# Mamba block with adaptive norms: layer norms on ScalarE, two additions on GpSimd, two PSUM banks in the last feed-forward, state sum two units behind the scans

## The chip, the cores and the metric

The kernel runs on one core of a Trainium2 chip. The metric is the device time of one launch in microseconds (us). The engines are TensorE (PE; its weight loads are listed as PEld), VectorE (DVE), ScalarE (ACT), GpSimd (POOL) and SyncE (SP), which issues the DMA transfers. Each runs its own instruction stream in order and waits for others by semaphores.

## The reference, cut to what matters

16 samples of 512 positions by 256 features go through a bidirectional Mamba block (512 channels, 64 states each) and a feed-forward, each with a scaled and shifted norm in front and a gate behind.

```python
h = layernorm(x) * (1 + ca) + sa
xn = layernorm(h, ln1)                          # the kernel's x_norm, then h_norm
x1 = mamba(xn, m1); x2 = flip(mamba(flip(xn), m2))
x = x + ga * (layernorm(x1 + x2, ln2) + xn)     # o_norm, then mix
n = layernorm(x) * (1 + cb) + sb                # n_norm
h = silu(n @ w1) * (n @ w2); h = gelu(h @ h1); h = gelu(h @ h2)
x = x + gb * (h @ w3)                           # W0, W1

# inside mamba, over t, for each of 512 channels and 64 states n:
h[t] = exp(dt[t] * A) * h[t-1] + dt[t] * x[t] * B[t]
y[t] = sum_n h[t] * C[t]
y = (y + xc * D) * silu(z)
```

## The kernel before, in words

The recurrence over time is one DVE instruction per 128 x 1024 values (`tensor_tensor_scan`). The work of a sample is cut into 128 **units**: two directions, four chunks of 128 channels, 16 groups of four states. A unit has two halves of 1024 values in a row. The samples follow each other as **bodies** of one program: `pre` (only the projections of sample 0), `first`, fourteen `mid` bodies (a loop), `last`, and `tail` (what is left of sample 15: output projection, norms, the whole feed-forward, no scans).

In each unit:

- ACT computes the decays `exp(dt * A)` of unit + 2 into one of four `state` slots (`decays`, L1034), and in two portions the products `v` for a later odd unit (`make_v`, L1047). POOL computes the last quarter of `v` (L1320).
- The driving term `driven` (a PSUM ring of two halves) comes from DVE for even units (`drive`, L1216) and from PE for odd units, by transposes of `v` (`drive`, L857). PE's transposes of a half wait for the scan of the same half of the unit before.
- DVE scans both halves in place (`scan`, L1227).
- POOL multiplies the scanned state by C (`read`, L1257).
- PE sums over n into `y_ps` (`accumulate`, L871). That frees the `state` slot: `decays` of unit + 2 wait for `summed` of unit - 2 (`slot_free`). At PE's unit u the code calls `accumulate(u - 1)` between the transposes of the two halves.
- SP loads the C rows, `ud` rows and weights.

After 16 units, DVE adds `xc * D` to `y_ps` (step `Y`, L1145), and the first `accumulate` of the next 16 waits for it.

All else (projections of the other direction and of the next sample, and norms and feed-forward of the previous sample) is laid out as **side steps** by a table: `side_steps` gives each step a unit, and each engine's `side` issues a step at the end of that unit. The step lists are per engine, so a step of engine A that needs one of engine B waits for B's count. A norm is four steps (`norm_steps`): `stats` (DVE, unit s), `aggr` (DVE, s + 1), `rstd` (POOL, s + 2, seven small instructions, L1274 to L1280), `norm` (DVE, s + 3, four `tensor_scalar` of 128 x 256, L1168). The four norms start at o: 8, n: 18, x: 64, h: 71. `x_scale` (L1172) and `x_shift` (L1174) follow at 68 and 69. `mix0` (L1177) and `mix1` (L1180) are DVE steps at 15 and 16. `W0` and `W1` (L1185 and L1188) are two DVE instructions each, at 76 and 127. The gates (POOL, L1288) are at 1 and 65.

The feed-forward works on 256 positions at a time with one PSUM bank, `q_ps`: PE fills it (L799 for F, L812 for H and G, L822 for W), ACT reads it (L1002, L1012), and `bank_free` holds PE's next step until ACT has read.

## Time and profile before

| what | value |
|---|---|
| median of 3 runs | 13444.66 us (13441.17 to 13444.91) |
| the profiled execution | 13442.57 us, of which the span is 13440.8 us |
| DVE busy | 12440.7 us (93%) |
| POOL busy | 11452.0 us (85%) |
| ACT busy | 10728.5 us (80%) |
| PE busy | 10269.7 us (76%), mean granted clock 0.877 |
| DMA | 1450 MB, about a third of the 16 engines' time |

The page gives busy time by engine; the windows view gives it by stretch; the list of waits says what ended an engine's idle time; the lines view groups instructions by source line; the timeline shows them in order. A timeline row is start, length, engine, line, operation, tiles, shape, count, and in brackets the idle time before it and what ended it.

### The profile page before, as it was taken

The page shows a single profiled execution, that of the slowest core. Times are in us where ns is not written, and L with a number is a line of the kernel's source. Part 1 is how long each engine was busy: PE and PEld are TensorE (multiplying, and loading weights), DVE is VectorE, ACT ScalarE, POOL GpSimd, SP SyncE. Part 2 cuts the span into 40 slices and gives each one's busy share as a digit, 9 for nine tenths or more (in the row PEclk, how much of TensorE's full clock was granted, in tenths as well). Part 3 has the DMA queues.
Part 4 walks back from the last instruction along what each step waited for, and adds up shares of the span by engine and source line. Part 5 has one row for each costly group of instructions (what it writes and reads, how often), then busy time and mean ns, then how long its engine had stood idle before and what let it go on. Part 6 is the DMA issues. An engine that isn't in the chain of part 4 may idle for free.

```text
span 13440.8 us, 178922 instructions
## 1 busy us (share of the span) xinstructions
PE 10269.7 (76%) x51228; PEld 5835.9 (43%) x51228; DVE 12440.7 (93%) x7383; ACT 10728.5 (80%) x23196; POOL 11452.0 (85%) x5812
## 2 busy tenths in 40 slices
PE   5567877778787787877878777787877878778776
PEld 2234444444344444434444444443444444344445
DVE  5999999999999999999999999999999999999991
ACT  5788878888887887878888788888878878788882
POOL 4898888888888888888988888888888888889892
PEclk7778988889898898988989888898988989889898
DMA  2223333333333333333333333333333333333332
GB/s 84 79 88 106 107 106 118 116 102 117 98 121 106 110 118 103 119 103 114 118 106 107 106 118 116 104 118 96 122 106 112 116 102 119 103 114 120 102 108 87
DMA packets 605372, 1450.00 MB, mean 108 GB/s; under 512 B 68400, under 2 KB 109504, under 8 KB 599792
## 3 DMA queue, kind: packets, MB, share of 16 engines
q1 hardware_dynamic: 604272, 1437.26, 32.8%
q8 instruction: 455, 7.45, 0.2%
q14 instruction: 645, 5.28, 0.1%
HBM read 1346.70 MB, written 90.31 MB: 107 GB/s over the span
## 4 chain that ended last, share of the span: by engine, by line
PE 26%; ACT 25%; issue 21%; DVE 17%; POOL 11%; DMA 0%; DVEq 0%; POOLq 0%; ACTq 0%; SPq 0%
DVE state L1227 9%; ACT v_sb L1047 8%; ACT state L1034 8%; PE driven L857 8%; POOL state L1257 8%; PE y_ps L871 5%; PE q_ps L812 5%; DVE driven L1216 3%; PE q_ps L799 2%; PE p_ps L720 2%; PE b_ps L847 1%; ACT L1034 1%; POOL v_sb L1320 1%; PE p_ps L728 1%; ACT hid L1017 1%
## 5 line engine op out<-in xcount | busy, mean ns | idle before, releaser
L1257 POOL TENSOR_TENSOR state<-state,c_rep 128x1024 f32<-128x1024 f32 x4096 | 9661.5, 2382 | 1544.2 <-DVE state L1227 1543.4
L1227 DVE TENSOR_TENSOR_SCAN state<-state,driven 128x1024 f32<-128x1024 f32 x4096 | 9105.9, 2270 | 462.7 <-PE driven L857 245.8
L1047 ACT ACTIVATE v_sb<-u_t,b_t 128x128 f32<-128x128 f32 x12288 | 3978.2, 505 | 1764.3 <-PE driven L857 1759.3
L1034 ACT ACTIVATE state<-ud_rep,cols_sb 128x512 f32<-128x512 f32 x8192 | 5175.6, 709 | 3.0 <-DMA ud_rep<-ud_rows 0.8
L857 PE MATMUL driven<-consts_sb,v_sb 128*128 128x128 f32 x16384 | 2700.5, 319 | 2119.8 <-DVE state L1227 2089.2
L857 PEld LDWEIGHTS driven<-consts_sb,v_sb 128*128 128x128 f32 x16384 | 2184.9, 164 | 3778.6 <-DVE state L1227 2605.4
L871 PE MATMUL y_ps<-state,consts_sb 128*32 128x512 f32 x16384 | 2523.6, 693 | 372.1 <-POOL state L1257 369.4
L1216 DVE TENSOR_TENSOR driven<-ud_rep,b_ps 128x1024 f32<-128x1024 f32 x2048 | 2390.0, 1212 | 17.0 <-DMA ud_rep<-ud_rows 17.0
L812 PE MATMUL q_ps<-hid,wq_sb 128*128 128x256 f32 x8192 | 2132.6, 406 | 241.1 <-ACT hid L1012 152.2
L812 PEld LDWEIGHTS q_ps<-hid,wq_sb 128*128 128x128 f32 x8192 | 1534.3, 197 | 982.8 <-issue 750.2
L1320 POOL TENSOR_TENSOR v_sb<-u_t,b_t 128x512 f32<-128x512 f32 x1024 | 1181.7, 1154 | 11.4 <-ACT u_t L963 11.4
L871 PEld LDWEIGHTS y_ps<-state,consts_sb 128*32 128x32 f32 x16384 | 341.9, 115 | 1178.2 <-issue 602.5
L728 PE MATMUL p_ps<-u_pad,dt_sb 128*128 128x512 f32 x1024 | 541.3, 655 | 40.7 <-ACT u_pad L939 40.2
L799 PE MATMUL q_ps<-xn_q,wq_sb 128*128 128x256 f32 x2048 | 529.5, 403 | 44.9 <-ACT hid L1002 40.5
L720 PE MATMUL p_ps<-x_t,wp_sb 128*128 128x512 f32 x1024 | 500.0, 611 | 24.1 <-ACT sz L983 12.5
L847 PE MATMUL b_ps<-b_parts,onehot 32*128 32x512 f32 x1024 | 517.7, 506 | 0.0
L799 PEld LDWEIGHTS q_ps<-xn_q,wq_sb 128*128 128x128 f32 x2048 | 378.0, 194 | 226.4 <-issue 125.6
L1012 ACT ACTIVATE hid<-q_ps,cols_sb 128x256 f32<-128x256 f32 x512 | 237.2, 463 | 293.8 <-PE q_ps L812 293.8
L822 PE MATMUL q_ps<-wq_sb,hid 128*128 128x256 f32 x1024 | 282.4, 424 | 51.8 <-ACT hid L1017 44.7
L728 PEld LDWEIGHTS p_ps<-u_pad,dt_sb 128*128 128x128 f32 x1024 | 192.1, 201 | 266.6 <-issue 197.5
L720 PEld LDWEIGHTS p_ps<-x_t,wp_sb 128*128 128x128 f32 x1024 | 187.3, 192 | 230.5 <-issue 135.6
L1304 POOL TENSOR_TENSOR hid<-hid 128x1024 f32<-128x1024 f32 x64 | 151.2, 2364 | 158.0 <-ACT hid L1006 158.0
(121 smaller groups left out, 5616.7 us busy)
## 6 DMA issues: line engine op xcount, KB each, us to landing
c_rep<-bc_rows SPq DMA_DIRECT2D x2048, 256.0 KB, 3.0
ud_rep<-ud_rows SPq DMA_DIRECT2D x512, 512.0 KB, 4.1
wq_sb<-in_h SPq DMA_DIRECT2D x512, 512.0 KB, 3.8
wq_sb<-in_f SPq DMA_DIRECT2D x128, 512.0 KB, 4.0
wp_sb<-in_win SPq DMA_DIRECT2D x64, 512.0 KB, 4.8
dt_sb<-conv_taps SPq DMA_DIRECT2D x32, 1024.0 KB, 5.6
ud_rows<-u_pad SPq DMA_DIRECT2D x128, 256.0 KB, 3.5
ud_rows<-dt_sb SPq DMA_DIRECT2D x128, 256.0 KB, 3.4
```

The costliest lines, as they stand in the source:

```text
L720: mm = pe.matmul(p_ps[:], wp_sb[:, m, k, :], x_t[:, k, :], start=(k == 0), stop=(k == DC - 1))
L728: mm = pe.matmul(p_ps[:], conv_w[:, m, k, :], u_pad[:, m, k:k + T], start=(k == 0), stop=(k == TAPS - 1))
L799: mm = pe.matmul(q_ps[:, which * TH:(which + 1) * TH], w[:, m % 2, which, k, :], n_t[:, k, i * TH:(i + 1) * TH], start=(k == 0), stop=(k = ...
L812: mm = pe.matmul(q_ps[:, 0:TH], w[:, k, :], src[:, k, :], start=(k == 0), stop=(k == HC - 1))
L857: mm = pe.transpose(driven[:, q % DRIVE_RING, j % 2, tt * P:(tt + 1) * P], v_sb[:, unit // 2 % V_RING, tt, j].rearrange("p e n -> p (e n)" ...
L871: mm = pe.matmul(y_ps[EG * j:EG * (j + 1), :], over_nn, state[:, k % STATE_RING, j, :], start=(g == 0), stop=(g == NG - 1))
L1034: ins = act.activation(state[:, unit % STATE_RING, j, :], ud_rep[:, nth % 2, j, 1, :], ACT.Exp, scale=a_neg[:, d, c, j, g:g + 1])
L1047: ins = act.activation(v_sb[:, unit // 2 % V_RING, tt, :, :, n].rearrange("p j e -> p (j e)"), u_t[:, nth % 2, tt, :], ACT.Identity, scale ...
L1216: dve.tensor_tensor(driven[:, h], u_rows(unit)[:, 2 * h:2 * h + 2], b_ps[:].unsqueeze(1).to_broadcast([P, 2, T]), ALU.mult).then_inc(dve_d ...
L1227: dve.tensor_tensor_scan(flat, flat, driven[:, q % DRIVE_RING].rearrange("p j t -> p (j t)"), 0.0, ALU.mult, ALU.add).then_inc(scanned, 1)
L1257: pool.tensor_tensor(part, part, c_rep[:, unit % ROW_RING, :].unsqueeze(1).to_broadcast([P, 2, T]), ALU.mult).then_inc(was_read, 1)
L1320: pool.tensor_tensor(v_sb[:, unit // 2 % V_RING, TT - 1].rearrange("p j e n -> p (j e) n"), u_t[:, nth % 2, TT - 1, :].unsqueeze(2).to_bro ...
```

## The change

- **Norms.** The four `norm` steps move from DVE to ACT, at the same units: four `activation(Identity)` per norm with `scale = rstd` and `bias = -mean * rstd`. POOL's `rstd` step has two more small instructions for that bias. `x_scale` and `mix` on DVE now wait for ACT.
- **Additions.** `x_q += o_sb` (was `mix1`, DVE, unit 16) becomes POOL's step `mixed` in unit 16; the second instruction of `W0` and `W1` becomes POOL's `add0` and `add1` in the same units. ACT's first F step waits for the addition, since it overwrites `hid2`; `n_stats` waits for `mixed`.
- **Two banks.** In the tail alone the feed-forward steps alternate between `q_ps` and `p_ps`, and `bank_free` looks two steps back.
- **Sum.** PE's unit u calls `accumulate(u - 2)`, always behind the transposes of the first half; bodies after the first one sum two units of the body before.
- **Y and gates.** `Y` steps and both gates come one unit later.

```diff
-    dve = [(s, part, name + "_stats", TT), (s + 1, part, name + "_aggr", TT), (s + 3, part, name + "_norm", TT)]
+    dve = [(s, part, name + "_stats", TT), (s + 1, part, name + "_aggr", TT)]
...
-    return [(s + 2, part, name + "_rstd", 7)], dve
+    return [(s + 2, part, name + "_rstd", 9)], [(s + 3, part, name + "_norm", TT)], dve
...
-        dve.append((NG * (c + 1), "o0", f"Y0{c}", 1))
-        dve.append((NG * (EC + c + 1), "o0", f"Y1{c}", 1) if c < EC - 1 else (0, "early", f"Y1{c}", 1))
-    pool.append((1, "early", "gate1", 2))
+        dve.append((NG * (c + 1) + 1, "o0", f"Y0{c}", 1))
+        dve.append((NG * (EC + c + 1) + 1, "o0", f"Y1{c}", 1) if c < EC - 1 else (1, "early", f"Y1{c}", 1))
+    pool.append((2, "early", "gate1", 2))
...
-    dve += [(MIX_AT + i, "early", f"mix{i}", 1) for i in range(2)]
+    dve.append((MIX_AT, "early", "mix", 1))
+    pool.append((MIX_AT + 1, "early", "mixed", 1))
...
-        dve.append((w_at + 4, part, f"W{i}", 2))
+        dve.append((w_at + 4, part, f"W{i}", 1))
+        pool.append((w_at + 4, part, f"add{i}", 1))
...
-    pool.append((NG * EC + 1, "o0", "gate0", 2))
+    pool.append((NG * EC + 2, "o0", "gate0", 2))
...
+        def q_bank(at, part, name):
+
+            if at.kind != "tail":
+                return q_ps
+            return (q_ps, p_ps)[[s[1:3] for s in PE_Q if at.has(s[1]) and s[3]].index((part, name)) % 2]
...
-                if j:
-                    p, n = steps[j - 1][1:3]
+                back = 2 if at.kind == "tail" else 1
+                if j >= back:
+                    p, n = steps[j - back][1:3]
...
-                    before_scans = unit == 0 and at.kind in ("mid", "last", "tail")
-                    to_drive, ends_pass = scans and unit + 1 in PE_UNITS, unit % NG == 0
+                    before_scans = unit < 2 and at.kind in ("mid", "last", "tail")
+                    to_drive, ends_pass = scans and unit + 1 in PE_UNITS, False
                     if to_drive and not ends_pass:
                         drive(at, unit + 1, 0)
-                    if before_scans or scans and unit:
-                        accumulate(at, unit - 1)
+                    if before_scans or scans and unit >= 2:
+                        accumulate(at, unit - 2)
...
+                if name.endswith("norm"):
+                    i = 0 if part == "next" else 1
+                    src, dst = {"o": (o_sb, o_sb), "n": (x_q, o_sb), "x": (xa, xa), "h": (xa, xa)}[name[0]]
+                    act.wait_ge(pool_side.sem, pool_side.done(at, part, name[0] + "_rstd"))
+                    for tt in range(TT):
+                        act.activation(dst[:, tt, :], src[:, tt, :], ACT.Identity, scale=rstd[:, i, tt:tt + 1],
+                                       bias=less_mean[:, i, tt:tt + 1]).then_inc(done, 1)
...
-                    elif name[2:] == "norm":
-                        dve.wait_ge(pool_side.sem, pool_side.done(at, part, kind + "_rstd"))
-                        for tt in range(TT):
-                            emit(dve.tensor_scalar(dst[:, tt, :], src[:, tt, :], mv[:, i, tt, 0:1],
-                                                   rstd[:, i, tt:tt + 1], ALU.subtract, ALU.mult), tt == TT - 1)
...
-                elif name == "mix1":
-                    dve.wait_ge(pool_side.sem, pool_side.done(at, "early", "pre2"))
-                    emit(dve.tensor_tensor(x_q[:], x_q[:], o_sb[:], ALU.add), True)
...
-                    dst = x_q[:, 2 * i:2 * i + 2, :]
-                    emit(dve.tensor_tensor(dst, dst, tmp, ALU.add))
...
+                    emit(pool.tensor_tensor(nb, mean, r, ALU.mult))
+                    emit(pool.tensor_tensor(nb, zero.to_broadcast([P, TT]), nb, ALU.subtract))
...
+                if name.startswith("add"):
+                    i = int(name[3])
+                    pool.wait_ge(dve_side.sem, dve_side.done(at, part, f"W{i}"))
+                    dst = x_q[:, 2 * i:2 * i + 2, :]
+                    pool.tensor_tensor(dst, dst, hid2[:, 0:2, :], ALU.add).then_inc(done, 1)
+                if name == "mixed":
+                    pool.wait_ge(done, pool_side.done(at, part, "pre2"))
+                    pool.wait_ge(dve_side.sem, dve_side.done(at, part, "mix"))
+                    pool.tensor_tensor(x_q[:], x_q[:], o_sb[:], ALU.add).then_inc(done, 1)
```

## Rows read from the trace of the kernel before

**Rows 1.** Windows: length, busy (count) of PE, PEld, DVE, ACT, POOL; clock; DMA

```profile
4000.00:8000.00 4000.00, 3108.72 (x15645) 1770.64 (x15647) 3816.74 (x2259) 3280.14 (x7082) 3505.19 (x1780) 0.88 0.34 111
...
5110.95:5117.85 6.90, 0.00 (x0) 0.00 (x0) 5.42 (x4) 4.52 (x8) 5.68 (x8) 0.58 0.04 14
```

**Rows 2.** Waits of DVE, then ACT, 4000 to 8000: total us, times, longest

```profile
DVE state L1227 <- PE driven L857: 68.4, 103, 1.5
DVE state L1227 <- ACT state L1034: 56.3, 45, 2.4
DVE o_sb L1168 <- POOL small L1280: 7.4, 5, 1.5
DVE xa L1168 <- POOL small L1280: 3.4, 5, 0.7
...
DVE state L1227 <- DVE x_q L1180: 1.0, 5, 0.2
...
ACT v_sb L1047 <- PE driven L857: 531.5, 124, 11.0
```

**Rows 3.** Lines of DVE, whole run: busy us, mean ns | idle before

```profile
L1168 DVE TENSOR_SCALAR xa<-xa,small 128x256 f32<-128x256 f32 x128 | 170.1, 1388 | 16.6 <-POOL small L1280 16.6
L1168 DVE TENSOR_SCALAR o_sb<-o_sb,small 128x256 f32<-128x256 f32 x64 | 82.6, 1349 | 24.7 <-POOL small L1280 24.7
L1188 DVE TENSOR_TENSOR x_q<-x_q,hid 128x512 f32<-128x512 f32 x32 | 65.4, 2044 | 1.1
L1168 DVE TENSOR_SCALAR o_sb<-x_q,small 128x256 f32<-128x256 f32 x64 | 59.3, 985 | 2.9 <-POOL small L1280 2.9
```

**Rows 4.** One source line (mix1) without the tail: ns min/median/max, first to last start

```profile
L1180 DVE TENSOR_TENSOR x_q<-x_q,o_sb x15: 2958/2969/2978, 1070.6 to 12489.3; 128x1024 f32<-128x1024 f32 x15
```

**Rows 5.** Timeline of a middle body, o_norm in unit 11

```profile
5112.40 5.42 DVE L1168 TENSOR_SCALAR o_sb<-o_sb,small 128x256 f32<-128x256 f32 x4 [1.45 <-POOL small L1280]
...
5120.19 1.97 PE L857 MATMUL driven<-consts_sb,v_sb 128*128 128x128 f32 x8 [10.37 <-DVE state L1227]
...
5125.92 2.29 DVE L1227 TENSOR_TENSOR_SCAN state<-state,driven 128x1024 f32<-128x1024 f32 x1 [1.43 <-PE driven L857]
```

**Rows 6.** Timeline of a pair of units without DVE side steps (34 and 35)

```profile
5260.39 8.81 DVE L1227 TENSOR_TENSOR_SCAN state<-state,driven 128x1024 f32<-128x1024 f32 x4
...
5263.16 1.04 PE L857 MATMUL driven<-consts_sb,v_sb 128*128 128x128 f32 x8
...
5263.65 2.55 ACT L1034 ACTIVATE state<-ud_rep,cols_sb 128x512 f32<-128x512 f32 x4
5264.14 1.07 PE L871 MATMUL y_ps<-state,consts_sb 128*32 128x512 f32 x8
...
5271.36 4.46 DVE L1227 TENSOR_TENSOR_SCAN state<-state,driven 128x1024 f32<-128x1024 f32 x2
```

**Rows 7.** A line of ACT in the stretch 4000 to 8000 us

```profile
L1012 ACT ACTIVATE hid<-q_ps,cols_sb 128x256 f32<-128x256 f32 x159 | 73.5, 462 | 49.1 <-PE q_ps L812 49.1
```

**Rows 8.** Lines of POOL, whole run

```profile
L1257 POOL TENSOR_TENSOR state<-state,c_rep 128x1024 f32<-128x1024 f32 x4096 | 9661.5, 2382 | 1544.2 <-DVE state L1227 1543.4
L1320 POOL TENSOR_TENSOR v_sb<-u_t,b_t 128x512 f32<-128x512 f32 x1024 | 1181.7, 1154 | 11.4 <-ACT u_t L963 11.4
L1276 POOL TENSOR_TENSOR small<-small 128x4 f32<-128x4 f32 x64 | 13.0, 204 | 5.0
```

**Rows 9.** Timeline of the tail: norm, mix, one F step, one H step, W

```profile
13172.35 1.38 DVE L1168 TENSOR_SCALAR o_sb<-o_sb,small 128x256 f32<-128x256 f32 x4 [2.89 <-POOL small L1280]
...
13175.02 1.23 DVE L1180 TENSOR_TENSOR x_q<-x_q,o_sb 128x1024 f32<-128x1024 f32 x1
...
13195.76 1.99 PE L799 MATMUL q_ps<-xn_q,wq_sb 128*128 128x256 f32 x8 [0.93 <-ACT hid L1002]
...
13236.21 3.72 PE L812 MATMUL q_ps<-hid,wq_sb 128*128 128x256 f32 x16 [0.56 <-ACT hid L1012]
...
13427.36 8.61 PE L822 MATMUL q_ps<-wq_sb,hid 128*128 128x256 f32 x32 [3.52 <-DMA wq_sb<-in_w]
```

More of the change, by code:

```diff
@@ L583, in store_xn @@
             def store_xn(at):
-                wait(dve_side.sem, dve_side.done(at, "next", "h_norm"))
+                wait(act_side.sem, act_side.done(at, "next", "h_norm"))
                 sp.dma_start(rows_of(xn_dram, at.b + 1), xa[:]).then_inc(xn_out.sem, 16)
@@ L599, in store_out @@
             def store_out(at):
-                wait(dve_side.sem, dve_side.done(at, "late", "W1"))
+                wait(pool_side.sem, pool_side.done(at, "late", "add1"))
                 sp.dma_start(rows_of(out, at.b - 1), x_q[:]).then_inc(out_stored.sem, 16)
@@ L705, in project @@
                         if part == "next":
-                            pe.wait_ge(dve_side.sem, dve_side.done(at, "next", "h_norm"))
+                            pe.wait_ge(act_side.sem, act_side.done(at, "next", "h_norm"))
                         else:
-                            pe.wait_ge(dve_side.sem, dve_side.before(at))
+                            pe.wait_ge(act_side.sem, act_side.before(at))
                     for tt in range(TT):
@@ L768, in network @@
             def network(at, part, name, quarter):
-                kind, n = name[0], name[1:]
+                kind, n, bank = name[0], name[1:], q_bank(at, part, name)
                 if quarter == 0:
@@ L784, in network @@
                     if k == 0:
-                        pe.wait_ge(dve_side.sem, dve_side.done(at, part, "n_norm"))
+                        pe.wait_ge(act_side.sem, act_side.done(at, part, "n_norm"))
                     for tt in range(TT):
-                        mm = pe.matmul(q_ps[:, tt * P:(tt + 1) * P], o_sb[:, tt, k * P:(k + 1) * P], ident,
+                        mm = pe.matmul(bank[:, tt * P:(tt + 1) * P], o_sb[:, tt, k * P:(k + 1) * P], ident,
                                        start=True, stop=True)
@@ L798, in network @@
                         for k in range(DC):
-                            mm = pe.matmul(q_ps[:, which * TH:(which + 1) * TH], w[:, m % 2, which, k, :],
+                            mm = pe.matmul(bank[:, which * TH:(which + 1) * TH], w[:, m % 2, which, k, :],
                                            n_t[:, k, i * TH:(i + 1) * TH], start=(k == 0), stop=(k == DC - 1))
@@ L811, in network @@
                     for k in range(4 * quarter, 4 * quarter + 4):
-                        mm = pe.matmul(q_ps[:, 0:TH], w[:, k, :], src[:, k, :], start=(k == 0), stop=(k == HC - 1))
+                        mm = pe.matmul(bank[:, 0:TH], w[:, k, :], src[:, k, :], start=(k == 0), stop=(k == HC - 1))
                 else:
@@ L995, in step @@
                     k = int(name[1])
-                    act.activation(n_t[:, k, :], q_ps[:], ACT.Identity, scale=mod_c[:, DC + k:DC + k + 1],
+                    act.activation(n_t[:, k, :], q_bank(at, part, name)[:], ACT.Identity, scale=mod_c[:, DC + k:DC + k + 1],
                                    bias=mod_c[:, k:k + 1]).then_inc(done, 1)
@@ L1000, in step @@
                     m = int(name[2])
+                    if m == 0 and (name[1] == "1" or at.kind != "first"):
+                        act.wait_ge(pool_side.sem, pool_side.done(at, "early", "add0") if name[1] == "1"
+                                    else pool_side.before(at))
                     for which, hid in enumerate((hid1, hid2)):
-                        act.activation(hid[:, m, :], q_ps[:, which * TH:(which + 1) * TH], ACT.Identity,
+                        act.activation(hid[:, m, :], q_bank(at, part, name)[:, which * TH:(which + 1) * TH], ACT.Identity,
                                        scale=scales[:, which, m:m + 1]).then_inc(done, 1)
@@ L1158, in step @@
                             dve.wait_ge(x_in.sem, x_in.done(at, "next", "x"))
+                        if kind == "n":
+                            dve.wait_ge(pool_side.sem, pool_side.done(at, "early", "mixed"))
                         for tt in range(TT):
```

41 lines of the change are left out of this document (23 added, 18 removed).

## The prediction, made before the result

> **What bounds the kernel now.** I read the windows first. In the stretch from 4000 to 8000 us DVE is busy for 3816.74 of 4000 us, which is 95.4%; POOL has 87.6%, ACT 82.0% and PE 77.7% [rows 1]. So DVE sets the pace there, and the rest of its time can be named: in the list of its waits, 68.4 us end with PE's transposes, 56.3 us with ACT's decays, 10.8 us with POOL's `rstd` [rows 2]. A middle body takes (12489.3 - 1070.6) / 14 = 815.6 us, by the first and the last start of an instruction that occurs once in a body [rows 4]. The stretch is therefore 4.90 bodies. Fourteen such bodies are 11,418 of the 13,441 us. The tail is another matter: there is no scan, and PE and ACT take turns at one bank [rows 9].
>
> An instruction taken from DVE is thus worth its whole duration, as long as the engine that gets it and the waits that it brings stay under DVE's new pace.
>
> **Norms, taken from DVE.** Per body (totals over 16): (170.1 + 82.6 + 59.3) / 16 = 19.5 us [rows 3]. The waits for `rstd` go too: 10.8 / 4.90 = 2.2 us [rows 2]. A norm also stops PE: its transposes wait for a scan, 10.37 us in the place shown, and then take 1.97 us where eight take 1.04 us elsewhere [rows 5, 6]; the granted clock of that pause is 0.58 of 2.4 GHz, nearer the 1.2 GHz level than the upper one [rows 1]. The slow transposes make the scan of unit 13 wait 1.43 us [rows 5]. I count that once per body. A DVE step that waits for its own last write leaves up to 0.2 us before the next scan [rows 2]; seven such waits go with the norms and additions, 0 to 1.4 us, and I take 1.2.
>
> **Additions, taken from DVE.** `mix1` takes 2.97 us [rows 4], and the second halves of `W0`, `W1` 65.4 / 16 = 4.1 us [rows 3]. Together DVE loses 19.5 + 2.2 + 1.4 + 1.2 + 3.0 + 4.1 = **31.4 us per body**.
>
> **What ACT gets.** Four ACTIVATE per norm. One of the same shape takes 462 ns [rows 7], so a norm is at least 1.85 us and four are 7.4 us per body. ACT waits 531.5 / 4.90 = 108 us per body for PE's transposes, in front of `v_sb` [rows 2]. That covers 7.4 us, in the mean. It is not everywhere: where ACT is behind, DVE waits for decays, 56.3 / 4.90 = 11.5 us per body [rows 2]. The norm on ACT also waits for `rstd` in front of the decays of the next unit. By the code those are due two units after they are issued. I cost it at nothing; with that cover gone it is 7.4 us.
>
> The Trainium skill speaks against this move: "ScalarE: Activation LUTs", Rules for kernel authors, gives additions and multiplications to VectorE. In the tail the row agrees, 4 tensor_scalar in 1.38 us against 1.85 us; beside GpSimd's work it does not, since there the same four take 5.42 us [rows 5, 9]. By that rule the norms would be a loss of some 0.5 us each, hidden or not.
>
> **What POOL gets.** One addition of 128 x 1024 and two of 128 x 512: at 2382 ns for 1024 values that is 2.4 + 2.4 us. Two small instructions more per norm at 204 ns plus 5.0 / 64 us between them: 8 x 0.28 = 2.3 us [rows 8]. Sum 7.1 us. POOL's busy time per body is 3505.19 / 4.90 = 715 us; it becomes 722, against a body of some 790 us: 91%. Per pair of units without side work POOL has 4 x 2.38 + 1.15 = 10.7 us (rather less back to back) against DVE's 5271.36 - 5260.39 = 10.97 [rows 6, 8]. So POOL recovers slowly from a burst. The worst one is at unit 66, where the gate (2 x 2.38 us, moved there) now stands in front of `x_rstd`, on POOL's queue: after the scan of unit 66, a last read 2.4, `v` 1.15, the gate 4.8, `rstd` with nine instructions 3.3, then ACT 1.85, 13.5 us in all. DVE reaches `x_scale` in unit 68 after two units, 2 x 4.4 + 2.3 = 11.1 us. That is a **new wait of 2.4 us**, queued behind it on DVE are the scans of unit 69, and for those PE and POOL wait. Other bursts, and DVE's remaining two-input operations beside a busier POOL, I bound by 0 and by 5 us per body (the `x_q` addition takes 1.23 us alone in the tail and 2.97 us in a body [rows 4, 9]; three further such operations could lose 1.7 us each) and take 2.5.
>
> The Trainium skill, "GPSIMD Engine Reference", Engine selection, says that an elementwise operation with two inputs is about twice as slow on GpSimd and belongs on VectorE. The tail agrees (1.23 us on DVE, 2.4 us by POOL's mean), so there the move costs. If it held on the path of the bodies too, the sum would lose the 7.0 us of the additions per body, about 100 us in all.
>
> **The sum two units behind.** Before, PE's `accumulate` stands between the transposes of the two halves and needs POOL's read of the unit before. Now it needs a read that is one unit older, so PE waits less for POOL; no row shows DVE gaining by it, and I take nothing. It has a price: a `state` slot comes free later, and ACT's decays wait for that. In the pair shown the decays start at 5263.65; with the sum of two units earlier in the place of this one, they would start when it ends, 5264.14 + 1.07 = 5265.21, that is 1.56 us later [rows 6]. Where ACT is behind anyway it comes later than that sum and loses nothing. DVE's waits for ACT's decays are 45 in 4.90 bodies, 9 per body, so the cost is between 0 and 9 x 1.56 = 14 us per body. Nearer the low end: ACT waits for PE in only 124 / 4.90 = 25 of a body's 64 pairs [rows 2]; in between it works without a pause, and a late start is then paid once for several waits of DVE, or by ACT's own next pause. I take **2.2 us**, one and a half times 1.56.
>
> **Y and gates later.** `Y` (0.7 us) only moves, and PE's next `accumulate` is later too. `gate1` at unit 2 ends 2.4 + 1.15 + 4.8 = 8.3 us after the scan of unit 2; PE's `O1a` waits for it at unit 3, with the transposes for unit 5 queued behind it. Those are due 4.4 + 2.3 + 4.4 = 11.1 us after that scan; `O1a` and one half take about 2 to 3 us. It just fits; if not, 1 us per body, inside the bound above.
>
> **A body** then saves 31.4 - 2.4 - 2.5 - 2.2 = **24.3 us**: 14 x 24.3 = 340. The first body has only x and h norms (10.6 + 0.7 us, less 2.4 and 1): 8. The last has o, n and the additions (8.9 + 1.5 + 7.0 + 1.4, less 4): 15.
>
> **Tail.** An F step takes 1.99 + 0.93 us, PE and then ACT; an H or G step 3.72 + 0.56 us [rows 9]. With two banks PE goes on. Between steps of one phase there are 7 intervals: F 2 x 7 x 0.93 = 13 (and up to 0.2 more each, as matmuls flow on); H and G 4 x 7 x 0.56 = 16, and up to 0.2 each by the same. Weights could hold this: PE waited 3.52 us for the last chunk [rows 9], and a slot's next chunk may be asked for only when its step is done, one step of 3.5 us ahead. That just covers it. The pair of N steps and the pair of O steps each lose one such gap, some 0.9 us: 2. I take 13 + 16 + 5 + 2 = 36, bounds 15 and 40. Against it: two norms on ACT (0.5 each), `rstd` (0.6 each), `mixed` 2.4 for 1.23, the adds 0.5 each: 4. Net 32, and the projection of sample 0 loses 2.
>
> **Sum.** 340 + 8 + 15 + 32 - 2 = 393. From the profiled 13442.6 us that gives 13,050; the median of the runs is 2 us above it, which is nothing here. **Predicted: 13,050 us.**
>
> **Rivals.**
>
> - *Nothing is lost elsewhere.* 31.4 us per body, 440 + 12 + 19, and 37 of the tail: 12,935. For it: POOL and ACT have room in the mean. Against it: DVE waits for them now. Chance 0.15.
> - *Half is eaten by new waits.* POOL is at 91% and late in bursts, ACT's backlog is paid five times: 12 us per body, 168 + 10 + 20: about 13,245, or 13,160 if the gain is 18 us. Chance 0.20.
> - *The norms only filled holes.* DVE's pauses gave POOL and ACT the time to catch up, and it now waits as long for `read` and decays: no gain in the bodies, 20 us in the tail. Speaks for it: POOL's 10.7 against 10.97 us. Against it: 108 us of ACT's and a tenth of POOL's time are idle. 13,425. Chance 0.04.
> - *Slower: the late sum starves ACT.* Place: `slot_free` in front of the decays. Price 1.56 us for each pair of units in which ACT has no room. It decides from 33 / 1.56 = 21 pairs of the 64 per body on. With 30 pairs: 47 us lost against 31.4, 15.6 us per body, some 218 us less the tail's 32: 13,630 (rounded). Against it: ACT must have been just in time in each of them, and only 9 waits per body show that. Chance 0.08.
>
> The forecast's own case (13,050, from 12,970 to 13,130) has 0.53. The range reaches from 12,925 to 13,260 and takes in the second and third case. A measurement of this kernel tells some 0.2% from no change. Faster by more than that: 0.88; within it 0.04; slower 0.08.
>
> **What would show it right or wrong.** No DVE row for the norms, body period near 791 us, DVE's busy share still about 95%. `x_scale` (DVE) waiting for ACT, some 2.4 us, once per body. DVE's waits for decays 11.5 us per body before: 14 if I am right, over 40 if the last rival is. F steps of the tail every 2 us, H every 3.5 to 3.7. If ACT waits at its decays for PE's `y_ps` in most pairs, but DVE not for ACT, the late sum costs nothing.

## The result, and the profile after

| | before | after |
|---|---|---|
| median (lowest to highest), same chip | 13443.57 us (13441.17 to 13444.91) | 13064.94 us (13057.31 to 13073.71) |
| profiled execution, its span | 13442.57, 13440.8 us | 13063.83, 13062.0 us |
| busy share of PE, DVE, ACT, POOL | 76, 93, 80, 85% | 78, 92, 83, 88% |

The ratio is 0.9719, with a 95% interval from 0.9702 to 0.9736: faster, 15 us from the forecast of 13,050.

Windows of the kernel after, with the columns of [rows 1]:

```profile
4000.00:8000.00 4000.00, 3171.38 (x16098) 1811.82 (x16097) 3769.79 (x2221) 3405.99 (x7382) 3639.71 (x1883) 0.90 0.35 113
...
5610.83:5621.46 10.63, 0.01 (x2) 0.01 (x1) 10.42 (x7) 6.10 (x17) 6.60 (x3) 0.64 0.05 8
```

DVE's share went from 95.4 to 94.2% [rows 1], although it has less to do: it waits more. Single lines of the kernel after, whole run or without the tail (ns min/median/max, first and last start): the step `mix`, which occurs once in a body, and the scan:

```profile
L1197 DVE TENSOR_TENSOR o_sb<-o_sb,mod_q x15: 1225/3030/5386, 1059.6 to 12146.2; 128x1024 f32<-128x1024 f32 x15
```

```profile
L1242 DVE TENSOR_TENSOR_SCAN state<-state,driven x4096: 2258/2262/2290, 171.5 to 12802.2; 128x1024 f32<-128x1024 f32 x196
```

A middle body takes (12146.2 - 1059.6) / 14 = 791.9 us, against 815.6 [rows 4]. The last scan starts at 12802.2, so the tail is 13062.0 - 12802.2 - 2.3 = 257.5 us; before, the last scan started at 13144.7 of 13440.8 and the tail took 293.8. From the starts of every 256th scan the span divides like this (us):

| | start | first body | 14 middle bodies | last body | tail |
|---|---|---|---|---|---|
| before | 167.7 | 791.8 | 14 x 815.66 | 768.2 | 293.8 |
| after | 171.5 | 791.4 | 14 x 791.67 | 758.1 | 257.6 |
| difference | +3.8 | -0.4 | -335.8 | -10.2 | -36.2 |
| foretold | +2 | -8 | -340 | -15 | -32 |

The same instructions of DVE also changed their durations. Three of them, over 128 x 2048 values, belong to the making of dt. First the kernel before, then after; columns as in [rows 3]. `rest` writes `u_pad`, `dt` writes `dt_sb`, `log1p` writes `sz`; the last line is `x_scale`:

```profile
L1197 DVE SCALAR_TENSOR_TENSOR u_pad<-sz,u_pad 128x2048 f32<-128x2048 f32 x32 | 141.7, 4428 | 55.2 <-ACT sz L975 55.2
L1203 DVE TENSOR_TENSOR dt_sb<-dt_sb,sz 128x2048 f32<-128x2048 f32 x32 | 116.9, 3653 | 1.1
L1201 DVE TENSOR_TENSOR sz<-sz,u_pad 128x2048 f32<-128x2048 f32 x32 | 81.2, 2536 | 36.5 <-ACT sz L978 36.5
```

```profile
L1212 DVE SCALAR_TENSOR_TENSOR u_pad<-sz,u_pad 128x2048 f32<-128x2048 f32 x32 | 91.8, 2870 | 52.2 <-ACT sz L992 52.2
L1218 DVE TENSOR_TENSOR dt_sb<-dt_sb,sz 128x2048 f32<-128x2048 f32 x32 | 97.0, 3030 | 1.1
L1216 DVE TENSOR_TENSOR sz<-sz,u_pad 128x2048 f32<-128x2048 f32 x32 | 95.8, 2993 | 55.5 <-ACT sz L995 55.5
L1191 DVE TENSOR_TENSOR xa<-xa,mod_p 128x1024 f32<-128x1024 f32 x16 | 19.9, 1244 | 36.5 <-ACT xa L939 36.5
```

Waits of DVE, of ACT and of PE in the kernel after, 4000 to 8000 us, as in [rows 2]:

```profile
DVE state L1242 <- PE driven L867: 97.4, 116, 2.7
DVE state L1242 <- ACT state L1054: 69.3, 50, 2.8
...
DVE xa L1191 <- ACT xa L939: 10.7, 5, 2.2
```

```profile
ACT state L1054 <- PE y_ps L881: 505.4, 204, 9.7
```

```profile
PE q_ps L790 <- POOL u_pad L1306: 17.5, 5, 3.7
```

The stretch holds 4000 / 791.9 = 5.05 bodies. Per body DVE waits 19.3 us for transposes (14.0 before), 13.7 for decays (11.5 before) and 2.1 for the norm in front of `x_scale`. The waits for `rstd` are gone. ACT's large wait is now at its decays, for PE's sum, and no longer at `v_sb`.

### The profile page after: what moved, and what is told of

Same layout as the page of the kernel before. It is cut to its first block, busy times and chain, and to the rows that moved or that the text cites. A ratio compares the mean times of both kernels' runs of the same rounds, so it can differ in the third digit from the quotient of the medians.

```text
span 13062.0 us, 179154 instructions
## 1 busy us (share of the span) xinstructions
PE 10161.7 (78%) x51228; PEld 5798.5 (44%) x51228; DVE 11974.4 (92%) x7080; ACT 10814.2 (83%) x23452; POOL 11547.6 (88%) x5988
## 4 chain that ended last, share of the span: by engine, by line
PE 28%; ACT 26%; issue 20%; DVE 17%; POOL 7%; DMA 1%; DVEq 0%; SPq 0%; POOLq 0%; ACTq 0%
DVE state L1242 10%; PE driven L867 9%; ACT state L1054 9%; ACT v_sb L1067 9%; PE y_ps L881 6%; POOL state L1272 4%; PE q_ps L822 4%; DVE driven L1231 3%; PE q_ps L809 2%; PE p_ps L730 2%; PE b_ps L857 1%; ACT L1054 1%; PE p_ps L738 1%; POOL u_pad L1306 1%; PE p_ps L754 1%
## 5 line engine op out<-in xcount | busy, mean ns | idle before, releaser
L1242 DVE TENSOR_TENSOR_SCAN state<-state,driven 128x1024 f32<-128x1024 f32 x4096 | 9103.8, 2270 | 561.9 <-PE driven L867 325.0
L822 PE MATMUL q_ps<-hid,wq_sb 128*128 128x256 f32 x7936 | 2031.1, 400 | 188.3 <-ACT hid L1032 109.0
L822 PEld LDWEIGHTS q_ps<-hid,wq_sb 128*128 128x128 f32 x7936 | 1463.3, 194 | 892.3 <-issue 699.3
L738 PE MATMUL p_ps<-u_pad,dt_sb 128*128 128x512 f32 x1024 | 511.6, 623 | 44.6 <-ACT u_pad L956 44.3
L775 PE MATMUL p_ps<-sz 16*128 16x512 f32 x256 | 181.8, 796 | 149.2 <-ACT u_pad L986 148.7
```

The source lines that it names most:

```text
L738: mm = pe.matmul(p_ps[:], conv_w[:, m, k, :], u_pad[:, m, k:k + T], start=(k == 0), stop=(k == TAPS - 1))
L822: mm = pe.matmul(bank[:, 0:TH], w[:, k, :], src[:, k, :], start=(k == 0), stop=(k == HC - 1))
L1242: dve.tensor_tensor_scan(flat, flat, driven[:, q % DRIVE_RING].rearrange("p j t -> p (j t)"), 0.0, ALU.mult, ALU.add).then_inc(scanned, 1)
```

## The experiments

Each was timed beside the kernel before, on the same chip as it. "The kernel after" as a base has 13,065 us. Body lengths are first and last start of `mix`, divided by 14, as above; per-unit figures are means over twelve middle bodies, from the starts and ends of the scans. A unit is counted from the start of its first scan to that of the next unit. An interval belongs to a ratio to the kernel before; two runs whose intervals overlap are not told apart by their times alone.

### The parts one by one

**Norms alone.** The kernel before, with the four `norm` steps on ACT and the two further small instructions on POOL.

```diff
-    return [(s + 2, part, name + "_rstd", 7)], dve
+    return [(s + 2, part, name + "_rstd", 9)], [(s + 3, part, name + "_norm", TT)], dve
```

> The kernel before with the four norms on ACT alone. By the forecast's terms a body loses 19.5 us of DVE work, 2.2 us of waits for rstd, 1.4 us of a wait behind slow transposes and 0.8 us of small gaps, and gets back at most 2.5 us: 21.4 us per body, in all about 13,130 us. The wait of x_scale should be near zero here, because the gate is in the unit before rstd. Rival: without DVE's pauses POOL falls behind and the early sum passes that on to PE and DVE at units 11 to 15 and 67: 15 us per body, about 13,225 us.

Measured: 13121.39 us, ratio 0.9762 (0.9745 to 0.9778), that is -320. The body is (12159.0 - 1039.0) / 14 = 794.3 us, 21.4 less. DVE's side work fell by 25.3 us and its waits rose by 3.3. The time is that of the forecast's terms; the wait of unit 13, of which the rival spoke, did rise, from 1.39 to 3.59 us. The tail is longer, 298.4 us against 293.8.

**Additions alone.** The kernel before with `mixed`, `add0` and `add1` on POOL.

```diff
-    dve += [(MIX_AT + i, "early", f"mix{i}", 1) for i in range(2)]
+    dve.append((MIX_AT, "early", "mix0", 1))
+    pool.append((MIX_AT + 1, "early", "mixed", 1))
...
+        pool.append((w_at + 4, part, f"add{i}", 1))
```

> The kernel before with the three additions on GpSimd alone. By the forecast a body loses 3.0 + 4.1 + 0.6 = 7.7 us of DVE's time; less 1 us of new waits, 15 bodies: about 13,340 us, the tail 2 us longer. Rival: the additions delay POOL at units 16, 76 and 127 and DVE's other operations meet them, and half of the gain goes: about 13,390 us.

Measured: 13301.94 us, 0.9895 (0.9879 to 0.9912), -140. The body is (12343.6 - 1063.8) / 14 = 805.7 us, 10.0 less, where the removed instructions account for 7.2. The rest is in other DVE instructions: `rest` takes 3651 ns on average in this run (4428 before), `dt` 3321 (3653), twice each in a body. The tail takes 297.7 us, 3.9 more.

**Banks alone.** The kernel before with `q_bank` in the tail, and in it a wait of `F10` for `W0` (the whole change has one for the addition there).

```diff
-                if j:
-                    p, n = steps[j - 1][1:3]
+                back = 2 if at.kind == "tail" else 1
+                if j >= back:
+                    p, n = steps[j - back][1:3]
...
+                    if name == "F10" and at.kind == "tail":
+                        act.wait_ge(dve_side.sem, dve_side.done(at, "early", "W0"))
```

> The kernel before with the two banks for the feed-forward of the tail, and nothing else of the change. Theory: the tail alone shortens, by the 36 us that it shortened with the whole change: 13,443 - 36 = about 13,407, F steps every 1.7 us and H and G steps every 3.5 us. Rival: part of the 36 us came from the norms and additions that the change moved off VectorE: 13,420 or above.

Measured: 13398.43 us, 0.9969 (0.9957 to 0.9980), -42. The last scan starts at 13140.5 of 13401.0, so the tail is 258.2 us: 35.6 less than before. The bodies are the same within 0.3 us.

**The late sum, with Y and the gates, alone.**

```diff
-        dve.append((NG * (c + 1), "o0", f"Y0{c}", 1))
+        dve.append((NG * (c + 1) + 1, "o0", f"Y0{c}", 1))
...
-                        accumulate(at, unit - 1)
+                        accumulate(at, unit - 2)
```

> The kernel before with the late sum, the later Y and the later gates alone. Theory A: it costs 2.2 us per body by the forecast, up to 7 us by the waits seen after the change: 13,475 to 13,550 us, with the new waits of DVE for ACT's decays at units 37 and 97 and for PE's transposes at units 1, 5, 17 and 113. Rival B: the late sum pays wherever POOL is more than 6.7 us behind, here 1.7 us at unit 11 and 0.9 us at unit 67: 13,400 to 13,445 us.

Measured: 13560.55 us, 1.0089 (1.0072 to 1.0106): +119, 11 us above the theory's range. The body is (12594.2 - 1074.2) / 14 = 822.9 us, 7.2 more. In 4000 to 8000 us, 4.86 bodies, DVE waits 77.2 us for decays, that is 15.9 per body against 11.5 before, and 81.0 us for transposes, 16.7 against 14.0.

**All but the late sum.** The kernel after, with sum, Y and gates where the kernel before has them.

```diff
-        dve.append((NG * (c + 1) + 1, "o0", f"Y0{c}", 1))
+        dve.append((NG * (c + 1), "o0", f"Y0{c}", 1))
...
-                        accumulate(at, unit - 2)
+                        accumulate(at, unit - 1)
```

> The changed kernel with the sum over n, the Y steps and the gates put back to where they were before (sum one unit behind the scans, Y at units 16, 32, ..., gates at 1 and 65); norms, additions and banks as changed. Theory A: the late sum and the later Y and gates only cost. In the changed kernel the waits of DVE that did not exist before sit at units 1, 5, 17, 37, 39, 42, 97 and 113 and add up to some 7 us per body, so this kernel should take about 12,960 us and its body 784 us. Rival B: POOL now runs up to 12 us behind the scans (unit 67) and 9 us (unit 11), and an early sum would hold PE's transposes until POOL has read the unit before, which hurts DVE from a lag of about 6.7 us on: then this kernel is slower than the changed one by 5 to 10 us per body, 13,140 to 13,215 us, and DVE's waits for PE's transposes near units 13 and 67 grow by 2 to 6 us.

Measured: 13003.14 us (12985.26 to 13005.16), 0.9670 (0.9654 to 0.9687). The late sum, with Y and gates, thus costs the whole change 62 us. The time lies between the theory's and the rival's. The rival's wait is there, 3.55 us at unit 13, but the kernel is faster all the same. Norms, additions and banks alone give 320 + 140 + 42 = 502 us, together 438. Of the difference of 64 us, 48 are in `rest`, `dt` and `log1p`: over the whole run DVE spends 33.1 us less in them with the norms alone and 22.3 less with the additions alone, but only 7.2 less with both (`rest` takes 3290, 3651 and 4167 ns). Of the late sum's 119 us half is left.

**Where the late sum loses.** It does what its code says. In the kernel with the early sum PE waits for POOL in front of the sum, and in the kernel after it doesn't; waits of PE, 4000 to 8000 us, early sum first:

```profile
PE y_ps L881 <- POOL state L1272: 174.1, 96, 8.8
```

```profile
PE y_ps L881 <- POOL state L1272: 2.2, 5, 0.5
```

DVE's waits say what it costs. With the early sum, same stretch, here 5.07 bodies:

```profile
DVE state L1242 <- PE driven L867: 94.2, 113, 4.0
DVE state L1242 <- ACT state L1054: 52.6, 47, 2.4
DVE sz L1216 <- ACT sz L995: 12.6, 6, 2.4
...
DVE xa L1191 <- ACT xa L939: 3.5, 5, 0.7
```

Per body the kernel after waits 3.3 us more for decays (13.7 against 10.4), 1.6 more in front of `log1p` (20.7 / 5.05 = 4.1 against 2.5), 1.4 more for the norm (2.1 against 0.7) and 0.7 more for transposes (19.3 against 18.6). In all its waits are 6.3 us longer per body and its side work is 3.4 us shorter (43.6 against 47.0), which leaves about the 3.2 us by which the body is longer (791.9 against 788.7).

The waits for transposes hide a give and take. At unit 13 the kernel after takes 2.4 us less. Where a pass of 16 units begins, it loses: the even units 0, 16, ... take 6.5 us less together, of which the eight `Y` steps are 5.9, and the odd ones behind them 10.7 us more, of which about 4 us are idle time. Three things differ there at once. `Y` is one unit later, the sum is one unit older, and its place on PE is another: in these eight units, and only there, the kernel before issues the sum in front of the transposes of both halves (`ends_pass` in the diff), and the kernel after between them. The timeline of the kernel after, unit 113:

```profile
5621.46 1.97 PE L867 MATMUL driven<-consts_sb,v_sb 128*128 128x128 f32 x8 [10.62 <-DVE state L1242]
...
5623.36 1.94 PE L881 MATMUL y_ps<-state,consts_sb 128*32 128x512 f32 x8
...
5625.22 1.97 PE L867 MATMUL driven<-consts_sb,v_sb 128*128 128x128 f32 x8
...
5627.23 2.29 DVE L1242 TENSOR_TENSOR_SCAN state<-state,driven 128x1024 f32<-128x1024 f32 x1 [1.47 <-PE driven L867]
```

The same place with the early sum:

```profile
5584.88 1.94 PE L881 MATMUL y_ps<-state,consts_sb 128*32 128x512 f32 x8 [8.74 <-POOL state L1272]
...
5586.75 1.92 PE L867 MATMUL driven<-consts_sb,v_sb 128*128 128x128 f32 x8
...
5588.93 1.09 PE L867 MATMUL driven<-consts_sb,v_sb 128*128 128x128 f32 x8 [0.25 <-DVE state L1242]
...
5589.72 4.46 DVE L1242 TENSOR_TENSOR_SCAN state<-state,driven 128x1024 f32<-128x1024 f32 x2 [0.21 <-DVE xc L1166]
```

PE pauses in both, 10.62 and 8.74 us, and is slow behind it: in the pause of the kernel after the granted clock is 0.64 of 2.4 GHz, nearer to the 1.2 GHz level (the window shown above), and eight transposes take 1.97 us, not 1.04 [rows 6]. With the early sum, the sum is done first, the second set takes 1.09 us, and `Y` stands in front of the scans: they wait for nothing but its write. In the kernel after all three run slowly one behind the other, and the second scan waits for the last. Such slow sets stand at three of the eight places (units 0, 16 and 112), where DVE waits 0.9 to 1.2 us for the transposes; with the early sum it waits for none there. By this PE's order and the pause cost there, and not the 0.7 us of the `Y` step, which is not in the pause; no run separates them.

**Gates back.** The kernel after, gates at units 1 and 65.

```diff
-    pool.append((2, "early", "gate1", 2))
+    pool.append((1, "early", "gate1", 2))
...
-    pool.append((NG * EC + 2, "o0", "gate0", 2))
+    pool.append((NG * EC + 1, "o0", "gate0", 2))
```

> The changed kernel with only the two gates put back to units 1 and 65, where the kernel before has them; Y and the sum over n stay late. Theory: with the gate at unit 2, the first product of O1 stands behind u and the scans of unit 5 wait 1.39 us, and with the other gate at unit 66 x_scale waits 2.13 us; both go, so some 3 us per body less, 15 bodies: 13,065 - 45 = 13,020, with the wait of VectorE at unit 5 under 0.3 us. Rival: the gate at unit 65 stands ahead of x_rstd on GpSimd, which then ends no earlier, and the wait at unit 5 is taken over by unit 3 or 4: 13,065, as before the edit.

Measured: 13046.61 us (13041.88 to 13059.77), 0.9710 (0.9694 to 0.9726): 18 us less, not 45, and the interval overlaps that of the kernel after. Units 3 to 5 give 1.0 us per body (21.16 to 20.14). Units 67 to 71 give nothing: 36.1 us in one, 36.4 in the other. The timelines around `x_scale`, the kernel after first:

```profile
5338.54 4.71 POOL L1306 TENSOR_TENSOR u_pad<-xc,sz 128x1024 f32<-128x1024 f32 x2
...
5348.61 1.25 DVE L1191 TENSOR_TENSOR xa<-xa,mod_p 128x1024 f32<-128x1024 f32 x1 [2.12 <-ACT xa L939]
```

```profile
5328.00 10.35 POOL L1272 TENSOR_TENSOR state<-state,c_rep 128x1024 f32<-128x1024 f32 x4
...
5331.67 2.11 DVE L1191 TENSOR_TENSOR xa<-xa,mod_p 128x1024 f32<-128x1024 f32 x1 [0.71 <-ACT xa L939]
...
5340.61 2.12 DVE L1193 TENSOR_TENSOR xa<-xa,mod_p 128x1024 f32<-128x1024 f32 x1
```

The wait falls from 2.12 to 0.71 us, but `x_scale` and `x_shift` take 2.11 and 2.12 us instead of 1.25 and 1.22. So this half of the theory fell: the wait was there, and its removal was worth nothing.

**x_scale one unit later.**

```diff
-        dve += [(s + 4, part, "x_scale", 1), (s + 5, part, "x_shift", 1)]
+        dve += [(s + 5, part, "x_scale", 1), (s + 6, part, "x_shift", 1)]
```

> The changed kernel with x_scale and x_shift of each body one unit later (69 and 70 instead of 68 and 69). Theory: x_scale waits 2.13 us for ScalarE's norm, which waits for GpSimd; one unit later the norm is there, VectorE's wait goes, and nothing else is bound by it: 15 bodies by 2.1 us, 13,065 - 31 = about 13,034. Rival: TensorE's transposes of x come later and a wait of their size appears there: 13,065.

Measured: 13058.46 us (13049.46 to 13061.36), 0.9715 (0.9698 to 0.9731): no difference from the kernel after that this measurement can tell. The rival's time came, not its mechanism. The wait is gone and units 67 to 71 are 1.6 us shorter (36.1 to 34.6); units 76 to 79 are 1.5 us longer (23.9 to 25.4). There POOL's last read of unit 76 ends 5.7 us after the scan, where it was 3.8: POOL hadn't caught up. What the scans of unit 79 wait for are PE's transposes, 2.7 us against 1.2 on average, and those stand behind an F step that waits for its weights:

```profile
5398.59 3.78 PE L809 MATMUL q_ps<-xn_q,wq_sb 128*128 128x256 f32 x8 [4.23 <-DMA wq_sb<-in_f]
...
5402.16 1.45 PE L867 MATMUL driven<-consts_sb,v_sb 128*128 128x128 f32 x8
...
5403.65 4.46 DVE L1242 TENSOR_TENSOR_SCAN state<-state,driven 128x1024 f32<-128x1024 f32 x2 [1.76 <-PE driven L867]
```

SP issues these weights 64.7 us after the start of unit 67 in both kernels, though DVE comes to unit 77 two us sooner: on SP's queue they stand behind C rows, whose slots come free by POOL's reads.

### The order of the sum and the transposes

**Sum behind both halves.** The kernel with the early sum; PE issues the sum after the transposes of both halves, not between them.

```diff
-                    if before_scans or scans and unit:
+                    if (before_scans or scans and unit) and (ends_pass or not to_drive):
                         accumulate(at, unit - 1)
...
+                        if unit and not ends_pass:
+                            accumulate(at, unit - 1)
```

> The changed kernel with the sum over n one unit behind the scans (as in the run with the early sum), but on TensorE that sum is issued behind both halves of the transposes and not between them. Theory: what VectorE waits for at unit 13 (3.55 us in the run with the early sum) is the second half of the transposes, which stands behind the sum over n, and that behind GpSimd's reads; with the sum behind both halves that wait falls to about 1.2 us and the other waits for transposes shrink: 2.5 to 4 us per body less than with the early sum, 13,003 - 50 = about 12,950. Rival 1: the wait is for the first half or for another thing, and nothing moves: 13,003. Rival 2: ScalarE gets y later, its decays fall behind and VectorE waits for them: slower than 13,003, up to 13,065.

Measured: 13060.81 us, 0.9720 (0.9703 to 0.9736), 58 us more than with the early sum: rival 2. But the parts differ. The first body takes 749.4 us instead of 779.2; the middle bodies 794.8 instead of 788.7. In these the wait of unit 13 (3.55 us) is gone altogether, as are those of units 3, 11 and 21 (0.8, 1.3, 0.9), and units 14, 28, 46, 84, 100 and 116 take 1.0 to 2.6 us more each. As the rival says, DVE waits longer for decays, 94.7 us in 4000 to 8000 against 52.6; for transposes it waits less, 53.1 against 94.2.

**In the first body alone.** The kernel with the early sum, this order in the first body only.

```diff
+                    behind = at.kind == "first" and not ends_pass
...
-                    if before_scans or scans and unit:
+                    if (before_scans or scans and unit) and not (to_drive and behind):
                         accumulate(at, unit - 1)
...
+                        if unit and behind:
+                            accumulate(at, unit - 1)
```

> As the run with the early sum, but with the sum over n behind both halves of the transposes in the first body alone. Theory: the first body has no feed-forward on TensorE, its transposes are late because they stand behind the sum and that behind GpSimd's reads, and it shortens by the 30 us of the run that has this order everywhere, with the other bodies as they were: 13,003 - 30 = 12,973. Rival: the first body's length was set by the order in the bodies after it, or the second body takes it back: 13,003.

Measured: 12977.29 us (12968.03 to 12980.64), 0.9653 (0.9638 to 0.9668), as the theory says. The first body takes 751.7 us, and the others stay within 2 us. The interval overlaps that of the early sum, but the four times are all below the lowest there, 12985.26 us.

**Where it gains**, in units 2, 10, 12 and 20 of the other bodies too.

```diff
-                    behind = at.kind == "first" and not ends_pass
+                    behind = (at.kind == "first" or unit in (2, 10, 12, 20)) and not ends_pass
```

> As the run with the early sum, but the sum over n is issued behind both halves of the transposes in units 2, 10, 12 and 20 of every body, and in all even units but the ends of passes in the first body. Theory: the order behind both halves gains where TensorE has little other work (units 3, 11, 13 and 21 lost 0.9, 1.4, 3.7 and 1.0 us of wait by it, the first body 30 us) and loses where it has much (units 28, 46, 84, 100 and 116 cost 1.0 to 2.6 us more). Taking it only where it gains: 4 to 7 us per body by 14 and 30 us of the first: 13,003 - 90 = about 12,915, with 12,880 to 12,950. Rival: the transposes of unit 13 come on time, but ScalarE's decays for unit 14 and 16, which follow TensorE's sum, take back what unit 13 gives (unit 14 cost 2.1 us more, 15 and 16 1.3 us): 0 to 2 us per body, 12,945 to 12,975.

Measured: 12959.74 us (12930.07 to 12973.65), 0.9643 (0.9630 to 0.9656). The times overlap with those of the run before, so a gain in the other bodies isn't shown. The profile is of the fastest execution, 12930.07 us; in it the body takes (12017.7 - 1016.2) / 14 = 785.8 us, 2.9 less than with the early sum. The time is in the rival's range, and so is the size of what comes back: unit 13 gives 3.7 us, and units 14 and 15 take 2.2 and 1.7. But most of that is waiting for transposes, not for decays. First the early sum, around unit 13:

```profile
4963.16 9.30 POOL L1272 TENSOR_TENSOR state<-state,c_rep 128x1024 f32<-128x1024 f32 x4
...
4967.88 1.93 PE L881 MATMUL y_ps<-state,consts_sb 128*32 128x512 f32 x8 [2.90 <-POOL state L1272]
4969.74 1.97 PE L867 MATMUL driven<-consts_sb,v_sb 128*128 128x128 f32 x8
...
4971.75 2.29 DVE L1242 TENSOR_TENSOR_SCAN state<-state,driven 128x1024 f32<-128x1024 f32 x1 [4.04 <-PE driven L867]
```

The same place with the sum behind the transposes, up to unit 15, where the old order holds again:

```profile
4923.65 1.97 PE L867 MATMUL driven<-consts_sb,v_sb 128*128 128x128 f32 x8 [1.09 <-DVE state L1245]
...
4930.11 4.46 DVE L1245 TENSOR_TENSOR_SCAN state<-state,driven 128x1024 f32<-128x1024 f32 x2
...
4937.25 1.94 PE L881 MATMUL y_ps<-state,consts_sb 128*32 128x512 f32 x8 [2.60 <-POOL state L1275]
...
4940.79 2.29 DVE L1245 TENSOR_TENSOR_SCAN state<-state,driven 128x1024 f32<-128x1024 f32 x1 [3.46 <-PE driven L867]
```

The chain is the same two times: POOL's reads are late, PE's sum waits for them, the transposes stand behind the sum, and DVE waits 3.5 to 4 us. It has only moved by a pair of units.

**Less load on POOL before that place.** As the last, with one or two of POOL's additions moved.

```diff
-    pool += [(Q_AT + i, "early", f"pre{i}", 1) for i in range(3)]
+    pool += [(at, "early", f"pre{i}", 1) for i, at in enumerate((Q_AT, Q_AT + 1, 14))]
```

> As the run with the sum behind both halves in some units, but one of GpSimd's full additions (x_q += xn_q, 2.36 us) moves from unit 9 to unit 14. Theory: what units 11 to 15 lose is GpSimd's backlog, in front of which the rstd step of unit 10 stands; its last read of unit 11 ends 10.3 us after the scan, and the order on TensorE only chooses where DVE pays. With 2.36 us less in front, the backlog of unit 11 is about 8 us and the waits of units 13 to 15 shrink by up to 2.4 us, so 1 to 2.4 us per body: 12,960 - 25 = about 12,935. Rival 1: the 2.36 us are paid in units 15 to 17 instead, where GpSimd gets them now: 12,960. Rival 2: the order on TensorE itself is what costs (its decays late at unit 14), and GpSimd's load doesn't matter: 12,960, with the waits at units 14 and 15 as they were.

Measured: 12939.60 us (12924.78 to 12948.82), 0.9626 (0.9613 to 0.9640). The interval overlaps that of the run before, 12959.74 us, and the profiled spans are 12937.8 and 12928.3, so a gain isn't shown. POOL's lag at unit 11 falls from 10.3 to 8.0 us, as the theory says, and unit 14 gives 2.0 us. Units 15 and 16 take back 0.8 and 1.4. The line of `mix` (unit 15, DVE) says how, first without and then with the moved addition (which stands in unit 14):

```profile
L1200 DVE TENSOR_TENSOR o_sb<-o_sb,mod_q x15: 2428/3108/4750, 1016.2 to 12017.7; 128x1024 f32<-128x1024 f32 x15
```

```profile
L1200 DVE TENSOR_TENSOR o_sb<-o_sb,mod_q x15: 1572/6586/7068, 1012.3 to 12020.9; 128x1024 f32<-128x1024 f32 x15
```

The median of `mix` doubles, from 3.1 to 6.6 us. In the profiled executions the bodies are no shorter (786.3 and 785.8 us), as rival 1 says.

With two moved additions:

```diff
-    pool += [(at, "early", f"pre{i}", 1) for i, at in enumerate((Q_AT, Q_AT + 1, 14))]
+    pool += [(at, "early", f"pre{i}", 1) for i, at in enumerate((Q_AT, 13, 14))]
```

> As the one before, but two of GpSimd's full additions move, from units 8 and 9 to units 13 and 14. Theory (backlog): 4.7 us less stand in front of the rstd step of unit 10, but the addition in unit 13 now stands in front of the reads of unit 14, while the norm's burst is just over: a further 0 to 1 us per body, 12,915 to 12,935. Rival: the second move only brings the backlog back at unit 14, and the time is above that of the run with one moved addition: 12,945 to 12,980.

Measured: 12983.39 us, 0.9660 (0.9646 to 0.9675): the rival, 3 us above its range. The lag at unit 11 is 7.2 us, at unit 15 it is 11.0, and in unit 16 DVE's `Y` waits 3.34 us for PE's sum.

## Why the prediction was right, point by point

- **DVE sets the pace, and what it loses is worth its duration: right.** The body fell by 24.0 us; 24.3 were foretold. DVE's share is 94.2%, foretold about 95.
- **31.4 us taken away: about right as a sum, with other terms.** DVE's side work fell by 32.0 us per body (75.6 to 43.6). The instructions that went are 28.5 of it by unit, not 26.6: I divided totals by 16 that include the cheap norms of the tail, 1.38 us for four [rows 9], and of sample 0 in front of the bodies. The wait at unit 13 (1.4 us) did not go, it is 1.20 against 1.39. What stops PE there is the scans that it waits for, not only the norm.
- **Contention, +2.5 us: wrong sign.** The instructions that stayed got shorter, by 32.0 - 28.5 = 3.5 us per body. `rest` alone accounts for (141.7 - 91.8) / 16 = 3.1. Unit 40 of the kernel before, then after:

```profile
5293.70 9.34 POOL L1257 TENSOR_TENSOR state<-state,c_rep 128x1024 f32<-128x1024 f32 x4
...
5299.81 6.39 DVE L1197 SCALAR_TENSOR_TENSOR u_pad<-sz,u_pad 128x2048 f32<-128x2048 f32 x1
```

```profile
5170.88 6.76 POOL L1272 TENSOR_TENSOR state<-state,c_rep 128x1024 f32<-128x1024 f32 x2 [1.42 <-DVE state L1242]
...
5172.81 2.61 DVE L1212 SCALAR_TENSOR_TENSOR u_pad<-sz,u_pad 128x2048 f32<-128x2048 f32 x1
```

  Before, four reads run back to back through it, at 2.3 us each, and DVE takes 6.39 us. After, DVE takes 2.61 and it is POOL's pair that takes 6.76 instead of 4.7. One of the two pays, and a shift of a microsecond or two decides which. In the whole change this gain goes with the late sum: with it alone the mean of `rest` is 2897 ns, with all but it 4167. But it does not belong to it alone, since the norms alone and the additions alone give 3290 and 3651.
- **x_scale waits 2.4 us: right as a size (2.1), wrong as a cost.** The wait is filled by the two instructions behind it, which run faster, and by POOL, which catches up; neither edit that removed it gained by that.
- **gate1 and O1a "just fits": wrong, by the 1 us that was stated.** PE waits for the gate 17.5 / 5.05 = 3.5 us per body, DVE 1.39 at unit 5; the gates moved back gave 1.0 us in units 3 to 5.
- **The late sum costs 2.2 us by late decays: right in kind, somewhat more in size.** DVE's waits for decays rose as foretold, from 11.5 to 13.7 us per body; against the kernel with the early sum they are 3.3 more. Of the sign for a sum that costs nothing, one half came (ACT waits at its decays for PE's sum 204 / 5.05 = 40 times per body, which has 64 pairs), the other, that DVE doesn't wait for ACT, did not. All in all late sum, `Y` and gates cost 3 us per body in the whole change and 7.2 alone. What the sum of terms lacked are waits in other places: in front of `log1p`, and where PE's order at the beginning of a pass changed. I looked at the sum's new place in the pair of [rows 6] alone, where it stood between the two sets before as well, and put the rest at "only moves". Shorter DVE instructions pay part of it.
- **ACT and POOL: right.** A norm of four instructions takes 2.07 us in the tail, against at least 1.85. In the bodies DVE waits for a norm of ACT at `x_scale` alone, and POOL at 91.0%, against 87.6 [rows 1], went with a faster body.
- **First body, -8: wrong, -0.4.** It gains its norms and loses about as much to the late sum, `Y` and gates: without these it takes 779.2 us. I had no term for PE's idle there. With no feed-forward to run, PE is busy 501 of 791 us in it, against 625 of 792 in a middle body; the order of sum and transposes alone moved this body by 30 us.
- **Tail, -32: right in direction, 4 us too little.** The banks gave 35.6 us, as foretold (36), by the run with them alone. The 4 us against it were not there: the whole change's tail is no longer than that run's (257.6 and 258.2). With one bank they are: norms alone and additions alone made the tail longer by 4.6 and 3.9 us. Why not with two stays open. The timeline of the tail:

```profile
12830.12 2.07 ACT L939 ACTIVATE o_sb<-o_sb,small 128x256 f32<-128x256 f32 x4 [33.23 <-POOL small L1298]
...
12851.57 1.89 PE L809 MATMUL q_ps<-xn_q,wq_sb 128*128 128x256 f32 x8
...
12853.30 1.89 PE L809 MATMUL p_ps<-xn_q,wq_sb 128*128 128x256 f32 x8
...
12892.22 3.69 PE L822 MATMUL p_ps<-hid,wq_sb 128*128 128x256 f32 x16 [0.17 <-DMA wq_sb<-in_h]
12895.74 3.62 PE L822 MATMUL q_ps<-hid,wq_sb 128*128 128x256 f32 x16
```

  F steps follow each other every 1.73 us (2.92 before), H steps every 3.5 (4.28), where the prediction said 2 and 3.5 to 3.7. The weights are just in time: 0.17 us of waiting here.

So the time is right to 15 us partly because two errors cancel. The prediction has DVE's side work fall by 26.6 - 2.5 = 24.1 us per body and its waits stay as they were (-2.2 - 1.4 - 1.2 + 2.4 + 2.2 = -0.2). The side work fell by 32.0, and the waits rose by 7.2, from 36.5 to 43.7. That the two errors are of one size is luck.

The rival by which the late sum makes it slower fell as a total, but its sign was right: late sum, `Y` and gates alone make the kernel slower by 0.9%, and part of that is DVE's longer wait for decays (4.4 of 7.2 us per body). What the Trainium skill says in "ScalarE: Activation LUTs", Rules for kernel authors (additions and multiplications to VectorE) would have kept the norms where they were; here VectorE was the bound, and the same arithmetic on ScalarE was worth 320 us.

**Still open.** What the later `Y`, the older sum and PE's order at the beginning of a pass cost by themselves was read from units and waits, not isolated. That POOL and DVE slow each other down follows from durations beside each other, in four places; no run changed that and nothing else. The fastest runs, 12,940 and 12,960 us, can't be told apart, nor can the second and 12,977.

## What to carry to other kernels

When one engine is busy for 95% of the time, an instruction taken off it can be worth its duration (the norms: 21.4 us off, the body 21.4 us shorter), even if it goes to an engine that is itself 80 to 90% busy. A wait in the profile is not a gain in waiting: where a backlog of a third engine is behind it, removing the wait moves the price on by some units (x_scale, unit 13, GpSimd's additions). What brought time here was another order on TensorE in the body where it pauses most; work taken from the engine with the backlog was not tried. A step that "only moves" changes an order: look at every kind of place where it stands, not at one pair, for who waits behind it and how long TensorE pauses there.

## What the runs showed of the hardware that was not expected

- One two-input instruction of VectorE over 128 x 2048 values takes 2.61 us or 6.39 us, with GpSimd's reads beside it both times. In the first case GpSimd pays, 6.76 us for a pair instead of 4.7. One over 128 x 1024 takes 1.22 us to 6.6 (median of `mix` with GpSimd's addition and reads in front of it).
- The scans and the drives, one input of which lies in PSUM, do not show this: the mean of 4096 scans is 2270 ns and that of a drive 1.21 us both before and after, with POOL busy 85 and 88% of the time.
